# A macaron block on one core: one list of steps for the whole run, q and k split at other places, the first stack issued from two queues, the last norms in halves

## What is computed

```python
def ffn(x):                        # 16 heads of 16, S = 1024
    q, k, v = split(x @ Wq), split(x @ Wk), split(x @ Wv)
    attn = softmax(einsum('bqd,bkd->bkq', q, k) / sqrt(D), axis=-1)
    z = merge(einsum('bkq,bkv->bqv', attn, v)) @ Wo
    z = l2_normalize(z)
    z = l2_normalize(z @ Wff)
    return gelu(z)
def attn(x):                       # 8 heads, linear
    q, k, v = heads(x @ w_qkv.T + b_qkv)
    return merge((q @ k.T) @ v) @ w_o.T + b_o
x = x + 0.5 * ffn(layernorm(x))
x = x + attn(layernorm(x))
x = x + 0.5 * ffn(layernorm(x))
```

## Time and profile before

| what | us |
|---|---|
| median of 3 runs | 3015.58 (3014.48 to 3017.93) |
| profiled execution, device time | 3017.08 |
| its span | 3015.3 |
| DVE busy | 2799.6 (93%) |
| PE busy | 2731.6 (91%) |
| ACT busy | 2721.6 (90%) |
| POOL busy | 901.7 (30%) |

### The profile page before, as it was taken

The page is one execution under the profiler, slowest core; times in us unless marked ns, Lnnn a source line. Parts: engine busy times, 40 slices in busy tenths (PEclk is TensorE's granted clock), DMA queues, the critical chain, the costliest instruction groups (busy, mean ns, idle before and its releaser), DMA issues.

```text
span 3015.3 us, 88294 instructions
## 1 busy us (share of the span) xinstructions
PE 2731.6 (91%) x36160; PEld 1100.9 (37%) x36160; DVE 2799.6 (93%) x5659; ACT 2721.6 (90%) x5028; POOL 901.7 (30%) x1195
## 2 busy tenths in 40 slices
PE   5989999999999999999999998989988888898987
PEld 2323343433434434344343433333333333333333
DVE  4999999999999999999999999999999899998996
ACT  2999898998999989999898989999998999999997
POOL 3332323323233232332323323222332223233232
PEclk8999999999999999999999999999999999999999
DMA  8222341233412334123341233433233343322332
GB/s 222 56 46 65 58 100 33 51 74 58 93 37 54 74 57 92 36 53 78 58 84 41 54 79 71 85 57 73 54 63 69 71 85 56 71 50 60 79 71 57
DMA packets 155254, 205.53 MB, mean 68 GB/s; under 512 B 34529, under 2 KB 88289, under 8 KB 154722
## 3 DMA queue, kind: packets, MB, share of 16 engines
q1 hardware_dynamic: 154594, 199.37, 31.8%
q0 software_dynamic: 256, 0.52, 0.1%
HBM read 46.66 MB, written 25.17 MB: 24 GB/s over the span
## 4 chain that ended last, share of the span: by engine, by line
DVE 32%; PE 30%; SPq 16%; issue 8%; ACT 7%; POOL 5%; DMA 2%; POOLq 0%; ACTq 0%; DVEq 0%
DVE exp_ring L657 27%; SPq L375 16%; PE ring L771 12%; PE ring L834 8%; PE o_acc L848 8%; ACT exp_ring L581 5%; PE ring L893 2%; DMA kq_stack<-kq_parts 1%; POOL kq_rest L362 1%; POOL kq_parts L366 1%; POOL kq_parts L360 1%; POOL kq_parts L364 1%; DVE w_xn L727 1%; DVE x_post L682 1%; ACT w_xn L593 1%
## 5 line engine op out<-in xcount | busy, mean ns | idle before, releaser
L657 DVE TENSOR_SCALAR_CACHE_REDUCE exp_ring<-ring 128x1024 f32<-128x1024 f32 x2048 | 2404.2, 1214 | 134.2 <-PE ring L834 129.8
L581 ACT ACTIVATE exp_ring<-exp_ring,neg_max 128x1024 f32<-128x1024 f32 x2048 | 2338.2, 1144 | 189.4 <-DVE exp_ring L657 188.1
L834 PE MATMUL ring<-kq_stack 128*32 128x512 bf16 x16384 | 1168.1, 384 | 131.7 <-DVE exp_ring L657 84.9
L848 PE MATMUL o_acc<-exp_ring,v_scaled 128*32 128x512 f32 x8224 | 1088.2, 604 | 86.2 <-POOL v_scaled L514 62.3
L834 PEld LDWEIGHTS ring<-kq_stack 128*32 128x32 bf16 x16384 | 413.3, 97 | 1045.8 <-DVE exp_ring L657 470.5
L514 POOL TENSOR_TENSOR v_scaled<-v_now,exp_rsums 128x64 f32<-128x64 f32 x513 | 152.4, 298 | 1763.0 <-DVE exp_rsums L672 1749.2
L581 ACT ACTIVATION_READ_ACCUMULATOR exp_ring<-exp_ring,neg_max 128x1 f32 x2048 | 385.1, 188 | 0.0
L848 PEld LDWEIGHTS o_acc<-exp_ring,v_scaled 128*32 128x32 f32 x8224 | 254.0, 111 | 311.1 <-POOL v_scaled L514 85.1
L771 PE MATMUL ring<-ffn_wo_wowff,o_T 128*32 128x256 f32 x4352 | 259.2, 380 | 7.8 <-DVE exp_ring L657 6.4
L771 PE MATMUL ring<-xn_T,ffn_wqkv 128*32 128x512 f32 x2112 | 261.8, 616 | 3.0 <-DVE exp_ring L657 1.9
L360 POOL TENSOR_TENSOR kq_parts<-kq_stage,zero 128x512 bf16<-128x512 f32 x130 | 142.6, 1097 | 176.9 <-DMA kq_stack<-kq_parts 101.6
(11 more groups left out here) (102 smaller groups left out, 1302.1 us busy)
## 6 DMA issues: line engine op xcount, KB each, us to landing
kq_stack<-kq_parts SPq DMA_DIRECT2D x2072, 64.0 KB, 2.4
x_post<-x_slots SPq DMA_DIRECT2D x17, 1024.0 KB, 5.7
x_prep<-x_slots SPq DMA_DIRECT2D x16, 1024.0 KB, 8.4
x_slots<-x_post SPq DMA_DIRECT2D x8, 1024.0 KB, 5.4
out<-x_post SPq DMA_DIRECT2D x8, 1024.0 KB, 4.7
x_prep<-in_L_attn_x SPq DMA_DIRECT2D x1, 1024.0 KB, 5.6
exp_ring<-in_L_attn_w_qkv SPq DMA_DIRECT2D x1, 512.0 KB
kq_stack<-kq_parts POOLq DMA_DIRECT2D x8, 64.0 KB, 3.6
```

Of the source, the lines that this page charges most:

```text
L581: nc.scalar.activation(e, e, ACT.Exp, bias=negmax[:, i % NM:i % NM + 1], scale=-1.0, accum_out=sums[:, g % EG, c:c + 1]).then_inc(exp_done, 1)
L657: nc.vector.tensor_scalar(E[:, (g % EG) * HQ + c, :].rearrange("p (b n) -> p b n", b=NB), ps, -1.0, None, ALU.mult, ALU.min, accum_out=neg ...
L834: last = mm(ps[k:k + COLS, n, :], kq[:, 0, c, j * P + k:j * P + k + COLS], kq[:, 1, c, n * BANK:(n + 1) * BANK], start=True, stop=True)
L848: last = mm(O[32 * c:32 * c + 32, n, :], vsc[a][:, g % EG, c, :], E[:, (g % EG) * HQ + c, n * BANK:(n + 1) * BANK], start=(a == 0 and j == ...
```

## The change

- **One list.** `TABLES` has four tables, START, PLAIN, LINEAR and TAIL. `put` places every step of the whole run with its phase, and `order` sorts it for each engine, SP too. Steps without work are not placed. The counts start from zero, so the 56 increments go, as do the memsets of zeroed buffers and the copy of x to DRAM: phases 0 to 7 load from the input.
- **Places.** In PLAIN the `qk` steps of the second half go from (9.2, 21.2, 37.3, 41.7) to (21, 28.8, 37.5, 41.1), those of the next phase from (73.3, 85.4, 93.6, 101.4) to (78.9, 84.8, 93.3, 102.4). POOL takes them half a tile later still. Nearly all other places move a little, in LINEAR mostly by less than two tiles.
- **Parts.** On PE a step may be cut into parts (`PARTS`). Only `gram` and `G` have a gap between parts (`GAP`, half a tile), so a `gram` is spread over 1.5 tiles.
- **Start.** x comes in two halves. Each of the 16 transposes waits for its own `xn`. Of the four first splits, three are made by ACT and DVE in turn (`FIRST_SPLITS`), straight from PSUM. Of the first stack's 32 DMAs SP issues 14 and POOL 18 (`BY_POOL`). The weights' transposes are PE steps with slots.
- **x1** comes in four chunks in place of two, on 128x512 values.
- **Tail.** The norms, `gelu` and the last store come in two halves, the first norm beside the last `u` steps.

```diff
-    PLAIN = {
-        "recip": 5.1, "av": 9.1, "av_next": 2, "z": 7.7,
-        "u": (14.5, 15.6, 16.8, 27.8, 33.6, 47.7, 53.4, 60.8),
-        "gelu": (67.1,),
-        "x1": (72.1, 72.2),
-        "xt": (61.7, 63.5),
-        "qk": (73.3, 85.4, 93.6, 101.4, 9.2, 21.2, 37.3, 41.7),
...
-    WITH_LINEAR = {
-        "gelu": (32.8,),
-        "x1": (36.1, 36.2),
-        "gram": (52.4, 58.3),
-        "xt2": (63.7, 94.9),
-        "qk": (77.8, 82.4, 93.7, 97.4, 31.4, 34.2, 38.7, 42.9),
...
+        "PLAIN": {
+            "recip": 5.7,
+            "av": 9,
+            "av_next": 2.5,
+            "z": 6,
+            "u": (8.5, 13, 16.4, 25.1, 32.5, 46.1, 55.5, 60.8),
+            "gelu": (70.2,),
+            "x1": (71.8, 72, 72.1, 72.2),
+            "xt": (62.1, 62.3),
+            "qk": (78.9, 84.8, 93.3, 102.4, 21, 28.8, 37.5, 41.1),
+            "stack1": (3.2,),
+            "stack2": (50.8,),
+            "stack3": (60.1,),
+            "stack0": (105.3,),
...
+        "LINEAR": {
+            "gelu": (32.6,),
+            "x1": (34.7, 35.4, 35.8, 36.6),
+            "gram": (52.4, 58.4),
+            "xt2": (66, 101.2),
+            "qk": (77.1, 81.7, 92.8, 97.6, 32.4, 35.9, 38.5, 42.5),
...
+        "TAIL": {
+            "u": (8.4, 10.7, 20, 27.6, 33.6, 51.2, 59.7, 60.2),
+            "u_norm": (23.8, 64.1),
+            "w_norm": (35.6, 68.8),
+            "gelu": (66.9, 90.5),
+            "x1": (79.8, 81.3, 90.5, 96),
...
+    PARTS = {"u": 2, "qk": 2, "v": 2, "y": 2, "gram": 4, "T": 3, "VK": 2, "G": 2, "H": 3}
...
+    GAP = {'gram': 0.5, 'G': 0.5}
+            "act": {"qk": 1.0, "u": 1.0, "xt2": 1.5, "gram": 1.5, "weights": 3.0, "G": 1.0, "xt": 0.5, "H": 1.5},
+            "dve": {"ln_stats": -1.0, "VK": -0.5, "H": 0.5, "z": -0.5},
+            "pool": {"recip": 0.5, "xn": 0.5, "x1": -1.5, "xbias": 2.5, "w_norm": 1.5, "qk": -0.5, "u_norm": -1}}
...
+                elif kind in PREP or kind in ("load_xp", "stack0"):
+                    if p + 1 < PHASES:
+                        put(at + place, kind, p + 1, i)
...
+                elif p >= 1:
+                    put(at + place, kind, p - 1, i)
+    def order(engine):
+        placed = []
+        for n, (place, step) in enumerate(steps):
+            kind = step[0]
+            parts, gap = PARTS.get(kind, 1), GAP.get(kind, 0)
+            place -= LEAD[engine].get(kind, 0)
+            if engine == "pe":
+                for part in range(parts):
+                    placed.append((place + gap * part, n, part, step))
+            else:
+                placed.append((place + gap * (parts - 1), n, 0, step))
+        return [(step, part) for _, _, part, step in sorted(placed)]
...
+                    if i % 4 == 0 and 2 * p + half > 0:
+                        q = (p, 0) if half else (p - 1, 2)
+                        for k in range(2):
+                            pool.wait_ge(stacked[k], stack_count(q[0], q[1] + k))
...
+                    nc.scalar.activation(hi, ps[:, 0, :], ACT.Copy, scale=qk_scale(i)).then_inc(first_hi, 1)
+                    act.wait_ge(first_rest, n)
+                    nc.scalar.activation(mid, resid[:, 1, :], ACT.Copy, scale=1.0).then_inc(first_mid, 1)
...
+                    nc.vector.scalar_tensor_tensor(out=resid[:, 1, :], in0=ps[:, 0, :], scalar=qk_scale(i), in1=hi,
+                                                   op0=ALU.mult, op1=ALU.subtract).then_inc(first_rest, 1)
+                    dve.wait_ge(first_mid, n)
+                    nc.vector.tensor_tensor(lo, resid[:, 1, :], mid, ALU.subtract).then_inc(first_lo, 1)
```

More of the change, by code:

```diff
@@ new lines, in build_macaron, with table, put @@
+    SP_STEPS = ("load_xp", "load_xr", "stack1", "stack2", "stack3", "stack0", "store")
+    PSUM_STEPS = ("tile", "u", "gram", "xt2", "T", "VK", "G", "H", "y", "xt", "qk", "v", "weights")
+    PARTS = {"u": 2, "qk": 2, "v": 2, "y": 2, "gram": 4, "T": 3, "VK": 2, "G": 2, "H": 3}
+    def table(p):
+        return TABLES["START"] if p < 0 else TABLES["TAIL"] if p == PHASES else \
+            TABLES["LINEAR"] if 1 <= p <= B else TABLES["PLAIN"]
+    steps = []
+    def put(place, kind, p, i):
+        steps.append((place, (kind, p, i)))
@@ new lines, in build_macaron @@
+    for p in range(-1, PHASES + 1):
+        at, places = p * TILES, table(p)
+        if 0 <= p < PHASES:
+            for t in range(TILES):
+                put(at + t, "tile", p, t)
+            for g in range(GROUPS):
+                put(at + HQ * g + places["recip"], "recip", p, g)
+                for n in range(NB):
+                    put(at + HQ * g + places["av"] + places["av_next"] * n, "av", p, g * NB + n)
+            for half in range(HALVES):
+                put(at + TILES // 2 * (half + 1) + places["z"], "z", p, half)
@@ new lines, in build_macaron, with ranks @@
+    ORDER = {e: order(e) for e in LEAD}
+    def ranks(engine):
+        found, n = {}, {}
+        for step, part in ORDER[engine]:
+            if part == 0:
+                n[step[0]] = n.get(step[0], 0) + 1
+                found[step] = n[step[0]]
+        return found
+    RANK = {e: ranks(e) for e in ORDER}
+    for kind in PARTS:
+        ends = [step for step, part in ORDER["pe"] if step[0] == kind and part == PARTS[kind] - 1]
+        assert ends == sorted(ends, key=lambda step: RANK["pe"][step]), kind
@@ L954 @@
+                if final and kind in ("u", "gram", "xt2", "T", "VK", "G", "H", "y", "xt", "qk", "v"):
+                    last.then_inc(filled[kind], 1)
 _INS = ['L0_attn_x', 'L0_attn_w_qkv', 'L0_attn_b_qkv', 'L0_attn_w_o', 'L0_attn_b_o', 'L0_ffn_Wq',
```

1129 lines of the change are left out of this document (548 added, 581 removed).

## The result

| | before | after |
|---|---|---|
| median, us | 3016.44 (3014.48 to 3017.93) | 2937.5 (2937.07 to 2938.12) |
| ratio to before | | 0.9739, interval 0.9722 to 0.9756 |
| span of the profiled execution | 3015.3 | 2936.3 |
| DVE, ACT, PE busy | 2799.6, 2721.6, 2731.6 | 2775.7, 2704.8, 2692.5 |

The account below looks back on a forecast made before the run. The prediction took DVE to bound linear phases, DVE and ACT together plain ones. Terms -16.0 - 11.7 - 33 - 16 - 6.5 - 3.5 = -86.7 from 3015.6 gave 2929 us, range 2892 to 2968.

Parts of the forecast that it names:

- Plain phases, -33: Phases 9 to 14: later splits find the stack landed, so 33 of 35.7 us of DVE gaps go.
- The gaps at 61 to 65: Plain phases: DVE gaps of 14.8 us, at the end of quarter 2's issue, stay and grow a little.
- Linear phases, -16: Phases 1 to 8: gram in parts shortens DVE's longest wait from 2.2 to about 0.7 us; -2 a phase.
- Start, -16.0: Up to tile 0: earlier load, halves, transposes one by one, relayed splits and a shorter stack save 16.0 us.
- The mis-sized term is the stack: Start: issuing bounds, so SP's 14 DMAs take 10.4 us beside POOL's 18 in 9.7; -6.0 us.
- POOL's DMAs are slow: Rival, first stack: each of POOL's 18 DMAs costs its cheapest split operation, stack 9 us later; 2938 us, chance 0.07.
- Phase 0, -11.7: Phase 0: 7.3 us of DVE work goes and stalls at 17, 73 and 81 go; 163.0 against 174.7 us.
- phase 15, -6.5: Phase 15: without the preparation of phase 16, ACT falls to 161.6 us; with 4.5 of slack, 166 us.
- Tail, -3.5: After the last tile: four gelu in place of eight, a shorter last x1 chunk and half the last store; -3.5 us.
- The floor: Rival: every place is better, linear phases give -40 and plain ones -48 us; 2890 us, chance 0.19.
- ACT's early steps: Slower rival, linear phases: ACT waits for PE at steps taken early, up to 10.8 us a phase; 3031 us, chance 0.03.
- Only the ends gain: Rival: in plain phases the gaps at 17 and 81 come back elsewhere; 2965 to 2980 us, chance 0.20.

Follow-up runs that it names:

- act_16: The kernel after with 16 of the first stack's 32 DMAs issued by ACT in place of 18 by POOL, ahead of ACT's weight copies; 2934.5 us.
- aligned: The kernel after with PLAIN's second-half splits at (21, 28.8, 33, 37) and 10 of the first stack's DMAs on POOL; 2944.7 us.
- best: The kernel after with second-half splits at (21, 28.8, 33, 37) in phases 0 and 15 only, 8 DMAs on POOL, 36 warm-up transposes on PE; 2934.3 us.

## Why the prediction was right, and where it was off

- **What bounds the kernel: right in the main.** In the plain phases the change takes idle time of DVE (-33.6 us) and adds 2.7 of work, in phase 0 and phase 15 it takes work (-6.4 and -7.2). In the linear phases, where only idle time was reckoned with, it took 8.2 of idle time and 6.4 of work.
- **Plain phases, -33: -30.9.** The cause is shown: with the old places the wait for the stack and the 176.7 us come back, and the new places alone bring 3.3 us a phase in the kernel before. `x1` behind `gelu` waits 9.3 us over the six phases, as much as the gap of 9.3 at 73 that had been set against it. DVE's idle time fell by 33.6, so the 33 came as told. The 2 us that are missing are work of DVE, 2.7 more, which had been put at nothing. Most of it is `x1` in four chunks: 24 operations of 687 ns in place of 12 of 1219, 1.9 us more. The gaps at 61 to 65 were to stay at 14.8 us or grow a little; 6.2 are left, of which the pair of `xt` has 0.84 a phase.
- **Linear phases, -16: -14.6.** The sum was right, and its reason carried a third of it (0.7 of the 1.9 us). That it came out near is partly luck: the parts of `gram` give all of the idle time that went, and the shorter operations of DVE, which nobody had reckoned with, the rest.
- **The half tile: costed at nothing outside PLAIN.** I named it only for the split at 21.5. In LINEAR it holds one split behind a scaling of v, and without it a linear phase takes 5.2 us more in each of eight phases.
- **Start, -16.0: -13.1.** SP begins the stack 12.4 us earlier, against 10.0 predicted for load, halves, transposes and splits (3.3 + 1.3 + 1.6 + 3.8). The load (3.3), halves and transposes (3.1) and splits (4.1) each came as told; 1.9 more are luck: in the profiled execution the clock had risen before the products, which took 7.07 us and not 8.92. **The mis-sized term is the stack: -0.7 in place of -6.0.** Its step was that issuing bounds at the rates of the rows: 14 x 0.74 on SP beside 18 x 0.54 on POOL. Issue on POOL did cost that (9.14 / 18 = 0.51). But SP's cost 1.23 each, since POOL's transfers hold it, and these take more of the DMA engines' time a KB. The kernel before had the sign: of SP's 24 DMAs, 20 are issued every 0.64 us or near it, and four, beside POOL's transfers, take 0.9 to 1.8. The mean of 0.74 hid that. I had also read 3.6 against 2.4 us to landing in the earlier trace rows as latency alone. And issue on a free second queue would not have given the 6 us either: in act_16 both queues were done after 10.7 us, the transfers bound, and the stack took 17.2. My rival "POOL's DMAs are slow" came near in size (+9 on this term; +5.3 measured), by another way. It let POOL's issue starve, as the Trainium skill's page "SBUF — State Buffer" (section "SBUF: two separate sides") has it beside DVE's copies. POOL's issue did not slow down at all. DVE made no copy from SBUF in that stretch, so no run here tests that rule. That this rival's time, 2938, is the one measured is luck too: of the 8 us by which the forecast was low, the whole start gives 2.9.
- **Phase 0, -11.7: -10.0, and phase 15, -6.5: -5.4.** The busy times that were to bound came within 1.2 us of those worked out (DVE in phase 0 159.2 for 158.3, ACT in phase 15 160.4 for 161.6). The gaps at 61 to 65 were told for the plain phases, "grow a little where the tiles now run faster", and put at nothing in these two. These two run fastest, and there the gap at 63 opens to 2.33 and 4.61 us. `aligned` and `best` show it for phase 15: with the splits four tiles earlier it takes 163.3.
- **Tail, -3.5: -5.0.** The power on four columns takes 1.01 us and not 1.65, and there are two in the chain; that I had given as a bound ("up to 1.5 earlier") and not as the value.
- **The rivals.** The floor was not reached, nor did ACT's early steps cost the linear phases: ACT waits for PE there 28.1 us over the eight, against 27.0 before, never over 1.0 at a time, and DVE waits less than before. "Only the ends gain" fell with 171.1 us a plain phase.

## What to carry to other kernels

In a list that an engine works through in order, look at what stands right behind a step that may wait: half a tile, which swaps a split and a scaling of v, was worth 42 us in the linear phases, and splits six to twelve tiles later, where the copy has landed, 52. A place that is right for one length of a phase is wrong for a shorter one, since issue from a queue takes its time in us and not in tiles; so phases that lose work want places of their own. Before a second queue is given more transfers, read how full the DMA engines are, what a packet of that queue costs, and whether the first queue still issues at its own pace beside it (one by one; a mean hides it). Queues share the engines, and only the idle time of these is to be had. And do not take the clock column at 1.00 near a launch for a record: compare the pace of the same instructions.
